# A graph network's count table: edge values stored from ACT in 112 + 13 rows, row gathers issued together, one-hots begun behind Pool's last issue

## What is computed

```python
def hop(h):                                   # L0 (2 hops) and, alike, L2 (16 hops) and L3 (2)
    return jax.ops.segment_sum(norm[:, None] * h[src], dst, num_segments=N)
def _egnn_conv(x, src, dst, edge_attr, W_msg, W_edge, W_root, b):   # L1, twice
    msg = x[src] @ W_msg + edge_attr @ W_edge
    agg = jax.ops.segment_max(msg, dst, num_segments=x.shape[0])
    return agg + x @ W_root + b
x = _layernorm(x + L0(x));  x = _layernorm(x + L1(x, edge_attr))
x = _layernorm(x + L2(x));  x = _layernorm(x + L3(x))
```

## Time and profile before

| what | value |
|---|---|
| three timed runs | 2411.85, 2416.16, 2422.86 us; median 2416.16 us |
| the profiled execution | 2425.24 us, of which the span of the trace is 2423.4 us |
| busy share of the span | PE 83%, DVE 50%, ACT 24%, Pool 34% |
| mean granted clock of PE | 0.906 of full speed |
| last instruction of the build stage | starts at 131.97 us |

### The profile page before, as it was taken

The page is one execution under the profiler, slowest core; times in us unless marked ns, Lnnn a source line. Parts: engine busy times, 40 slices in busy tenths (PEclk is TensorE's granted clock), DMA queues, the critical chain, the costliest instruction groups (busy, mean ns, idle before and its releaser), DMA issues. The chain is left out here.

```text
span 2423.4 us, 46254 instructions
## 1 busy us (share of the span) xinstructions
PE 2009.7 (83%) x18497; PEld 1663.2 (69%) x18497; DVE 1203.4 (50%) x3354; ACT 583.8 (24%) x1505; POOL 833.8 (34%) x742
## 2 busy tenths in 40 slices
PE   3688468888888448888888459999999999999868
PEld 3678435555555325555555349999999999999758
DVE  6934535555655325555565464444444444445436
ACT  4843201111111101111111123333323333332231
POOL 6433267777774447677677400000000000000000
PEclk9799779989999659999999779999999999999879
DMA  2034344555554235555455400000000000000000
GB/s 71 1 84 117 97 107 127 136 129 132 138 130 124 67 87 131 129 137 136 130 137 138 111 5 2 2 2 1 2 2 2 1 2 2 2 1 2 1 3 21
DMA packets 145659, 160.47 MB, mean 66 GB/s; under 512 B 42813, under 2 KB 130245, under 8 KB 145070
## 3 DMA queue, kind: packets, MB, share of 16 engines
q1 hardware_dynamic: 93165, 81.77, 13.0%
q0 software_dynamic: 22128, 34.74, 7.7%
q10 hardware_dynamic: 30152, 41.02, 4.7%
HBM read 101.66 MB, written 55.75 MB: 65 GB/s over the span
## 5 line engine op out<-in xcount | busy, mean ns | idle before, releaser
L1130 POOL DMA_INDIRECT c_gathered<-messages,idx_all x624 | 668.1, 1071 | 277.3 <-issue 175.5
L1161 PE MATMUL c_taken<-c_hot,rows 125*96 125x512 f16 x1300 | 521.9, 401 | 32.0 <-issue 30.5
L1162 PE MATMUL c_taken<-c_hot,rows 125*96 125x512 f16 x1300 | 519.2, 399 | 20.3 <-issue 19.2
L764 PE MATMUL l_ps<-rows,counts 125*128 125x192 f16 x5625 | 471.1, 247 | 65.3 <-DVE rows L808 65.1
L764 PEld LDWEIGHTS l_ps<-rows,counts 125*128 125x128 f16 x5625 | 466.7, 98 | 68.5 <-issue 64.7
L764 PE MATMUL l_ps<-l_u,counts 125*128 125x192 f16 x5625 | 470.4, 247 | 9.5 <-DVE l_uf L828 5.0
L764 PEld LDWEIGHTS l_ps<-l_u,counts 125*128 125x128 f16 x5625 | 467.8, 98 | 10.8 <-DVE l_uf L828 5.5
L1199 DVE TENSOR_SCALAR c_hot<-c_offset_srcs 125x512 f16<-125x512 f16 x1300 | 293.9, 289 | 146.7 <-remote 68.7
L1253 ACT ACTIVATE c_back<-c_tr 128x384 f32<-128x384 f32 x208 | 102.1, 491 | 808.2 <-PE c_tr L1170 237.5
L828 DVE SCALAR_TENSOR_TENSOR l_uf<-l_ps,l_cf,l_wide 125x96 f32<-125x96 f32 x400 | 127.0, 318 | 328.8 <-ACT l_wide L783 328.8
L1161 PEld LDWEIGHTS c_taken<-c_hot,rows 125*96 125x96 f16 x1300 | 168.6, 130 | 158.4 <-issue 69.6
(11 more groups left out here) (255 smaller groups left out, 1517.6 us busy)
## 6 DMA issues: line engine op xcount, KB each, us to landing
running_max<-c_back ACTq DMA_DIRECT2D x208, 192.0 KB
c_attr<-attr_halves SPq DMA_DIRECT2D x412, 64.0 KB
c_mask<-segment_mask SPq DMA_DIRECT2D x206, 96.0 KB
c_gathered<-messages,idx_all POOLq DMA_INDIRECT x624
l0a_raw<-in_ea_t SPq DMA_DIRECT2D x34, 195.3 KB
c_srcs<-sources SPq DMA_DIRECT2D x50, 128.0 KB
attr_halves<-l0a_hi SPq DMA_DIRECT2D x34, 97.7 KB
attr_halves<-l0a_lo SPq DMA_DIRECT2D x34, 97.7 KB
```

What stands on the lines that cost most here:

```text
L764: last = pe.matmul(ps[:, t % HB, 0:2 * F], at[:, k, t * P:t * P + 128], u[hop % 2][:, k, :], start=(k == 0), stop=(k == T - 1))
L1130: pool.indirect_dma_start(out=gat[:, i % 2, j, :], out_offset=None, in_=c["y_d"], in_offset=bass.IndirectOffsetOnAxis(ap=idx_all[:, i * IT ...
L1161: pe.matmul(bank_of(i, GG), y[:, t, 0:F], one_hot, start=(t == 0), stop=False)
L1162: last = pe.matmul(bank_of(i, GG), y[:, t, F:2 * F], one_hot, start=False, stop=False)
```

## The change

Five edits, all in `build_counts`. The loads of `di` and `si` are split into 112 and 13 rows and shared between SP and ACT. ACT converts `si` into `srcf`, in DVE's place. ACT stores `ev`, in 112 and 13 rows; the store of `pad` has a semaphore of its own, which only the last window waits for, and goes ahead of the wait for `ev` that SP no longer has. Pool issues all five row gathers first and then the five windows, and then increments a new semaphore `s_asked`. DVE makes `begin` 3 and 4 ahead of its main loop, and waits there for `s_asked`. ACT does all `signs_of` before `keys_of(0)`.

```diff
             def _(sp):
-                half = P // 2
-                sp.dma_start(di[0:half, :], dst_v[0:half, :]).then_inc(s_dst, 16)
-                sp.dma_start(si, src_v).then_inc(s_src, 16)
+                sp.dma_start(di[0:WHOLE, :], dst_v[0:WHOLE, :]).then_inc(s_dst, 16)
+                sp.dma_start(si[WHOLE:P, :], src_v[WHOLE:P, :]).then_inc(s_src, 16)
...
-                sp.wait_ge(s_ev, 1)
-                sp.dma_start(ev_flat[0:3 * E].rearrange("(p c) -> p c", p=P), ev.rearrange("p c a -> p (c a)")).then_inc(s_edges, 16)
                 sp.wait_ge(s_pad, 1)
-                sp.dma_start(ev_flat[3 * E:3 * E + P * PADS].rearrange("(p c) -> p c", p=P), pad).then_inc(s_edges, 16)
+                sp.dma_start(ev_flat[3 * E:3 * E + P * PADS].rearrange("(p c) -> p c", p=P), pad).then_inc(s_padded, 16)
...
                 pool.wait_ge(s_at_row, 1)
-                row(0)
-                row(1)
-                row(2)
+                for g in range(GN):
+                    row(g)
                 pool.wait_ge(s_edges, 32)
-                window(0)
-                row(3)
-                window(1)
-                row(4)
-                for g in range(2, GN):
+                for g in range(GN):
+                    if g == GN - 1:
+                        pool.wait_ge(s_padded, 16)
                     window(g)
+                pool.sem_inc(s_asked, 1)
                 pool.wait_ge(s_ceil, 6)
...
             def _(act):
-                half = P // 2
-                act.dma_start(di[half:P, :], dst_v[half:P, :]).then_inc(s_dst, 16)
+                act.dma_start(di[WHOLE:P, :], dst_v[WHOLE:P, :]).then_inc(s_dst, 16)
+                act.dma_start(si[0:WHOLE, :], src_v[0:WHOLE, :]).then_inc(s_src, 16)
...
+                act.wait_ge(s_src, 32)
+                act.copy(srcf, si).then_inc(s_srcf, 1)
+                act.wait_ge(s_ev, 1)
+                for ps in (slice(0, WHOLE), slice(WHOLE, P)):
+                    act.dma_start(ev_flat[0:3 * E].rearrange("(p c) -> p c", p=P)[ps, :],
+                                  ev[ps, :, :].rearrange("p c a -> p (c a)")).then_inc(s_edges, 16)
                 act.wait_ge(s_less, 1)
-                for g in range(3):
+                for g in range(GN):
                     signs_of(g)
                 keys_of(0)
-                signs_of(3)
-                signs_of(4)
...
-                v.wait_ge(s_src, 16)
-                ch(v.tensor_copy(srcf, si))
+                v.wait_ge(s_srcf, 1)
...
                 begin_of(2)
+                begin_of(3)
+                begin_of(4)
                 v.wait_ge(s_idx, 1)
                 v.tensor_copy(c["idx_all"][:, :], ps_misc[:, 0:NE_T]).then_inc(s_idx_out, 1)
+                v.wait_ge(s_asked, 1)
...
-                    if t == 0:
-                        begin_of(3)
-                        begin_of(4)
```

More of the change, by code:

```diff
@@ L247, in build_counts @@
             sem(f"b_{n}") for n in ("turned", "keys", "hot", "pe", "flush", "digit", "by_f", "idx", "idx_out", "ceil", "clear"))
+        s_padded, s_asked, s_srcf = (sem(f"b_{n}") for n in ("padded", "asked", "srcf"))
         (s_gate, s_step, s_load, s_hot2, s_bank2, s_added, s_tri, s_end, s_sq, s_root, s_edges, s_less) = (
```

## The result

Over 20 runs of each, the changed kernel takes 2415.01 us (2407.55 to 2422.80) and the kernel before 2423.33 us (2411.85 to 2439.35). The ratio is 0.9964, with a 95% interval of 0.9949 to 0.9978: 8.7 us less, between 5.3 and 12.4. The forecast was 12.9 us less, 0.53%, and 2403.3 us. The time lies outside the range of 2397 to 2412. Of the 11.7 us by which it missed, 7.2 are the base: the three runs shown had a median of 2416.16, twenty have 2423.33. The other 4.5 us are a gain that is smaller than the sum (the two medians lie 8.3 us apart).

A forecast was written before the change was run, and what follows sets the result against it. DVE was taken to set the pace of the count build. Gains of 5.5 (first one-hot), 7.09 (stall) and 0.26 (begin 3 and 4) sum to 12.85, say 12.9 us: 2416.16 - 12.9 = 2403.3 us, range 2397 to 2412.

The forecast's parts named there:

- What bounds, and why the stall is there: Build loop: DVE sets the pace; Pool's window 3, issued into DVE's one-hot chain, is held until DVE pauses; stall 7.09 us.
- The head: Ahead of L510: `di` split into 112 and 13 rows removes DVE's idle 1.06 us.
- Pool's order and the stores: Ahead of the loop: stores land at 13.3; Pool's own queue sets window 0 at 13.66, window 4 at 18.66.
- The first one-hot: DVE's loop start: at 19.75 us, set by the wait for `s_asked`, 5.5 us earlier.
- begin 3 and 4: DVE's main loop, tile 0: moving them ahead takes 0.26 us out of the loop.
- ACT's lag: Key copies at tiles 4, 5 and 6: 2.7 us more ACT work, costed at nothing, at most 1.5 us.
- the tail: Behind the loop, through Pool, PE and DVE, 124.09 to L586 at 129.07: stays, with the same instructions.
- The stall: DVE's idle time in the loop, 53.16 to 60.25: all windows out before DVE starts, so 7.09 us go.
- The semaphore: Rival, chance 0.12: `s_asked` fires too early, window 4 is blocked, 4.9 us lost; gain 8.0, time 2408.2.
- The data: Rival, chance 0.14: row gathers or stores land as late as before; gain 9.9 or 8.1, time 2406.2 or 2408.1.
- the sign of 16: Profile sign of late data: `begin` 3 or 4 late, or window 0 behind 16 us.
- the clock: Rival, chance 0.04: PE's lower clock early in the hops; 0.5% slower after 50 us; sign: share below 0.92.

The follow-up runs named there:

- the pause put in by hand: Kernel before, DVE's tile 2 also waiting for PE's first bank of tile 1: 2273.40 against 2278.26 us, ratio 0.9978; without graph operation L1, mean 1280.2 us.
- the half without the early rows: Kernel before with only the split loads, ACT's cast of `si` and ACT's stores of `ev`; Pool's order as before: ratio 0.9985.
- the delayed one: Changed kernel with 31 small DVE instructions ahead of the first one-hot, 12.7 us in all: ratio 1.0000 to the kernel before.
- without L1: Kernels without the graph operation holding the two edge convolutions; means over ten runs: before 1284.6 us, changed 1274.4 us.
- the first four experiments: Changed kernel rerun, 0.9970; only loads, cast and stores, 0.9985; only Pool's order, early `begin` and wait, 1.0005; changed without DVE's `s_asked` wait, 0.9963.
- the order alone: Kernel before with only Pool's new issue order, `begin` 3 and 4 ahead of the loop and the `s_asked` wait: ratio 1.0005.
- the kernel with the new semaphores: Kernel before plus three semaphores and three Pool increments of them that nobody waits for: ratio 0.9986.

## Why the prediction was half right

*What bounds, and why the stall is there:* right. The blocked issue and DVE's pause go together in every profile, and the pause put in by hand shows it. Too general was only that no Pool instruction gets through DVE's chain (L362 to L364 above).

*The base:* this term was off by 7.2 us. The sum starts from 2416.16, the median of three runs, and twenty have 2423.33. With that base the same gain would have given 2410.4, inside the range, and with the old base and the measured gain 2407.5, inside too: it took both errors to leave it, and the base is the larger. That the three runs lay low was chance, and the range had allowed 4.3 us for it.

*The head:* 1.06 us taken, 1.11 measured (L510 at 4.90). `ev` was ready at 9.13 (9.21 taken).

*Pool's order and the stores:* window 0 at 13.99 (13.66), window 4 at 19.00 (18.66). In the changed kernel Pool did not wait for the stores. In the half without the early rows it did, until 14.07, 4.9 us behind their issue at 9.16, where the sum took some 4. In the first profile of the changed kernel Pool's queue sets window 0 (row 4 ends at 13.68, and the next issue follows 0.30 us later); in the delayed one it is the stores, at 14.12. The two bounds lie within 0.2 us of each other.

*The first one-hot:* 19.92 (19.75), but by the keys, 5.93 us behind window 0 and not 5.34, and not by the wait for `s_asked`.

*begin 3 and 4:* tile 0 now takes 23.38 - 19.92 = 3.46 us, 0.24 less (0.26). *ACT's lag* never reached DVE, and *the tail* stayed, with 5.06 us of wait ahead of its DVE step (4.98).

*The stall:* this step failed, in its size. "7.09 us go" is right for the execution that was profiled. But the term belongs to a pause of DVE that an execution has or has not. Where it has it, the kernel before is already 6.4 us quicker (131.6 to 125.2), and the change is worth only 12.1 - 6.4 = 5.7 us, with 12.1 the distance of the mean ends, 131.7 (five profiles of the whole kernel before) and 119.6 (four of the changed one, two of them without L1). With four of ten runs of that kind, without L1, the mean gain is 12.1 - 0.4 x 6.4 = 9.5 us, and 10.2 were measured. The whole program's 8.7 (5.3 to 12.4) fits with a share between none and all.

It also fits the chip of the first four experiments if the stall was seldom there, in before and in the stores-only kernel alike. Then one expects 5.7 us less for the change, 6.1 less without the wait, 5.6 less for the stores alone and 0.7 more for the order alone. Measured were 7.3, 9.0 and 3.6 us less and 1.2 more, each interval holding its number. With the stall in every execution of before, 5.8 us less for the order alone lies outside its interval, and so do 12.1 less for the stores alone, if those never have the stall. This is an argument from times: no profile of the kernel before was taken on that chip.

*The rivals:* none of mine was this one. The semaphore was not too early: no window issue is long, and without the wait at all DVE found window 4 already begun. The data did not come late: window 0 at 13.99 is ahead of the sign of 16, and window 4 at 19.00 was not kept waiting for its `begin`. Of the clock, the sign did show in the first profile: over the first 106.4 us of the hops the granted clock was 0.90, under the 0.92 of before, beside the 3.4 us lost there; in the second profile it was 0.92 and nothing was lost. I had asked what could go wrong in the changed kernel, and never whether the profile of before was typical.

What stays open: that the whole kernel's missing 4 us are executions without the stall is argued, not shown. In the whole kernel before I have seen only profiles with the stall, five of five, and the kernel with the new semaphores makes six; were four of ten executions without it, six in a row with it would have a chance of 0.6^6, about 5%. The split is seen without L1. On how many executions of which chip it holds isn't known. The profiles do say where the later stages scatter. From the first hop of L2 to the end all whole-kernel profiles take 1003.4 to 1005.3 us. From the first hop to the convolutions they take 161.6 to 164.1, but for the 166.0 named above. The two convolutions take 1118.6 to 1123.1 in four profiles of before on one chip, and 1126 to 1144 in four kernels on another. So a loss of a few us in the convolutions can't be excluded.

## What to carry to other kernels

A stall that hangs on a race between two engines is not a constant. Before you put it into a sum, take several profiles, and ask what small delay would make it vanish. A wider scatter of the runs is a hint that one profile can't give: 8.8 us over ten runs before, 4.3 changed and 1.7 with the short pause, all without L1. In the whole kernel the convolutions scatter by as much, and the hint is weak. Let an engine that issues indirect DMAs go first, or give it a gap of half a microsecond: a wait that was added gained 5 us. And a median of three runs lay 7.2 us from that of twenty here, nearly as much as the 8.7 us of the change.

## What was not expected of the hardware

- A Pool instruction behind a chain of f16 TENSOR_TENSOR on DVE is held over the ends of many of DVE's instructions, 14 of them in the earlier trace rows, and gets through in a pause of 0.39 us. Its neighbour behind it was then held only 1.9 to 2.2 us, in DVE's next instructions and without a pause, and three TENSOR_SCALAR of Pool 3.2 to 3.8 us each; why, I can't say. In the delayed kernel two window issues (17.89 and 19.21 us) fall among DVE's 31 small TENSOR_SCALAR, each of which waits for the one before, and took 1.02 and 1.13 us: they were not held.
- PE's pace changed by a factor of 1.8 (0.45 to 0.25 us per bank) at 32.8 us in one execution and 41.4 in another of the same build. The granted clock reads 1.00 over both stretches, as in these windows of the execution with the pause and then of the first profile of before:

```profile
33.00:35.00 2.00, 2.00 (x25) 2.00 (x23) 2.00 (x2) 1.96 (x5) 2.00 (x1) 1.00 0.00 0
```

```profile
33.00:35.00 2.00, 2.00 (x32) 1.79 (x29) 2.00 (x2) 2.00 (x5) 2.00 (x1) 1.00 0.00 0
```

  25 matmuls against 32 in the same two microseconds: a granted clock of 1.00 doesn't say that PE runs at full pace.
- The same two convolutions took 977 us on one chip (1267.2 - 290.2) and 1124 on another.
